# Two-layer AdaLN block on one core: the routing of the first expert stage in smaller pieces, and another order at the first expert tile

## What is computed

```
h = layernorm(x) * (1 + cb) + sb
logits = h @ w_router.T                    # 8 experts
probs = softmax(logits); vals, idx = top_k(probs, 2)
gates = sum(one_hot(idx) * vals)
acc = gelu(h @ Ws1.T + bs1) @ Ws2.T + bs2  # shared expert
acc = acc + sum_e gates[e] * (gelu(h @ W1[e].T + b1[e]) @ W2[e].T + b2[e])
x = x + gb * acc / sqrt(1.25)
```

## Time and profile before

| | |
|---|---|
| runs, us | 971.08, 972.5, 970.03 |
| profiled execution, us | 971.25, its span 969.4, granted clock 0.915 |
| busy in the span | PE 85%, DVE 77%, ACT 63%, POOL 49% |
| attention / first feed-forward / rest | to 480 / 480 to 720 / from 720 |
| chain that ended last | PE 44%, DVE 21%, POOL 13%, issue 11%, ACT 6% |
| mean of one: activation L1307, rounding L1313, subtraction L1442 | 689, 632, 739 ns |
| rank matmuls L459, 16 in all | 386 ns median |
| pieces of the chain: L1028 x2, L1033 x8, L1017 x4 | 1.05, 1.09, about 0.6 us |

### The profile page before, as it was taken

How to read it: one execution, slowest core, us unless ns; L and a number is a source line. 1 busy time by engine, 2 the same in 40 slices (tenths; PEclk the granted TensorE clock), 3 DMA queues, 4 the chain that set the end, 5 groups by cost and what they waited for, 6 DMA issues and landing times.

```text
span 969.4 us, 14044 instructions
## 1 busy us (share of the span) xinstructions
PE 825.5 (85%) x4566; PEld 438.3 (45%) x4566; DVE 746.9 (77%) x1560; ACT 614.3 (63%) x1097; POOL 477.8 (49%) x783
## 2 busy tenths in 40 slices
PE   5499999999988988797896999899962937899996
PEld 4232223323312222222374777787751525676664
DVE  6598888888899878882277688878839776999971
ACT  1128888888867867576385677667733754576541
POOL 4702564737366666346364067775658308314221
PEclk9659999999999999899599899999987957899998
DMA  6834736475647374202104166666533100000001
GB/s 200 189 85 154 177 122 167 131 157 146 142 124 166 112 179 112 86 24 106 62 29 170 35 242 213 232 220 205 189 120 145 26 8 1 0 1 1 1 34 54
DMA packets 45076, 110.77 MB, mean 114 GB/s; under 512 B 7806, under 2 KB 20606, under 8 KB 39494
## 3 DMA queue, kind: packets, MB, share of 16 engines
q1 hardware_dynamic: 39436, 98.33, 34.6%
q0 software_dynamic: 4992, 10.36, 3.1%
q10 hardware_dynamic: 576, 1.19, 0.4%
HBM read 57.65 MB, written 51.03 MB: 112 GB/s over the span
## 4 chain that ended last, share of the span: by engine, by line
PE 44%; DVE 21%; POOL 13%; issue 11%; ACT 6%; DMA 3%; SPq 1%; POOLq 0%; ACTq 0%; DVEq 0%
PE PS L1073 11%; POOL yd L1278 9%; PE PS L1062 8%; PE PS L1046 6%; DVE mx L896 5%; DVE cb L2334 3%; PE PS L1028 1%; PE PS L319 1%; PE PS L1083 1%; PE PS L320 1%; PE PS L321 1%; PE PS L2429 1%; PE PS L1017 1%; POOL Gl L1270 1%; ACT E L808 1%
## 5 line engine op out<-in xcount | busy, mean ns | idle before, releaser
L896 DVE TENSOR_REDUCE mx<-PS 128x2 f32<-128x1024 f32 x256 | 305.5, 1220 | 60.4 <-PE PS L1046 58.5
L808 ACT ACTIVATE E<-PS 128x512 f32<-128x512 f32 x512 | 272.4, 597 | 70.7 <-PE PS L1062 66.5
L1062 PE MATMUL PS<-Q,K 51*128 51x512 bf16 x512 | 167.6, 399 | 15.4 <-ACT E L808 7.3
L1046 PE MATMUL PS<-K,Q 48*128 48x512 bf16 x512 | 144.2, 413 | 27.2 <-DVE mx L896 15.7
L1073 PE MATMUL PS<-E,V 128*18 128x512 f32 x1024 | 142.1, 629 | 0.0
L1062 PEld LDWEIGHTS PS<-Q,K 51*128 51x128 bf16 x512 | 37.5, 95 | 175.9 <-ACT E L808 98.8
L1278 POOL DMA_INDIRECT yd<-yt,goes x92 | 96.1, 1045 | 42.3 <-issue 23.7
L1442 DVE TENSOR_TENSOR Gl<-Gf,Gh 128x512 fp32r<-128x512 f32 x117 | 84.7, 739 | 25.7 <-ACT Gh L1313 21.4
L510 POOL DMA_INDIRECT xs<-HT,pos x64 | 64.0, 1001 | 72.6 <-ACT E L808 41.3
L1307 ACT ACTIVATE Gf<-PS,WR 128x512 f32<-128x512 f32 x92 | 63.3, 689 | 42.1 <-PE PS L321 30.4
L2334 DVE SCALAR_TENSOR_TENSOR cb<-ye,gt,cb 128x128 f32<-128x128 f32 x224 | 62.4, 356 | 0.0
(11 more groups left out here) (421 smaller groups left out, 1830.6 us busy)
## 6 DMA issues: line engine op xcount, KB each, us to landing
WR<-wsd SPq DMA_DIRECT2D x23, 1028.0 KB
xs<-zero SPq DMA_DIRECT2D x8, 2112.0 KB, 7.2
wsd<-wsp SPq DMA_DIRECT2D x8, 1024.0 KB, 4.1
Q<-dqk SPq DMA_DIRECT2D x16, 384.0 KB
K<-dqk SPq DMA_DIRECT2D x16, 384.0 KB
HT<-xs SPq DMA_DIRECT2D x23, 264.0 KB
dqk<-SPL SPq DMA_DIRECT2D x31, 192.0 KB, 2.8
stage<-in_w SPq DMA_DIRECT2D x9, 516.0 KB
```

The lines of the kernel that those rows point to most:

```text
L808: e.activation(E[:, m % 4, n % 4], PS[:, bank["exp", n], :], ACT.Exp).then_inc(*k.inc("exp", n))
L896: e.tensor_reduce(mx[:, 2 * s % 96:2 * s % 96 + 2], PS[:, o:o + 2, :], AX.X, ALU.max, negate=True).then_inc(*k.inc("max", s))
L1046: return e.matmul(PS[:, o + n % 2, :], Q[r, b % 3, h // 2, qt * P:(qt + 1) * P], K[r, b % 3, h // 2, :], start=True, stop=True)
L1062: e.matmul(PS[:, o, :], K[r, b % 3, h // 2, kt * P:(kt + 1) * P], Q[r, b % 3, h // 2, :], start=True, stop=True).then_inc(*k.inc("exp_mm", n))
```

## The change

Routing functions are cut into pieces of one to three operations, and the pieces get steps of their own. The operations are fewer: subtracting the best logit comes first, so that "is the best" is a comparison with zero joined to the weighting; the second mask is added to the first by TensorE's accumulation; running totals carry over from group to group inside the scan, by one more element per expert that is zero in the mask `one`. The groups become 16, 8, 4 and 4 tiles (before: 12, 8, 8, 4). Group 0 is routed in batch 5 (before: 4), group 1 in batch 7, steps 14 to 26 (before: 6), group 2 in batch 7 from step 42. Scatters: tiles 0 to 7 in batch 6 and 8 to 21 in batch 7 (before: six in 5, six in 6, eight in 7, two at its end). At the first expert tile SyncE loads one weight set, waits for the scatters, loads the tokens, then the other two weight and token sets; its transposes move from step (5, 3) to (6, 1), and both roundings two steps later.

```diff
-GROUP0 = {0: (0, 12), 1: (12, 20), 2: (20, 28), 3: (28, 32)}
+GROUP0 = {0: (0, 16), 1: (16, 24), 2: (24, 28), 3: (28, 32)}
+        def dve_best_a(e, k, g):
+            L, w, a, c = group(g)
+            k.wait_ge("lgt", c // 4 - 1)
+            chain(k, e.tensor_reduce(w[:, 4, :, 0], L, AX.X, ALU.max))
+            e.tensor_tensor(L, L, over8(w[:, 4, :, 0]), ALU.subtract).then_inc(*k.inc("v"))
+        def dve_best_b(e, k, g):
+            chain(k, e.scalar_tensor_tensor(w[:, 2], L, 0.0, desc(w), ALU.is_ge, ALU.mult))
+            chain(k, e.tensor_reduce(HT[:, a:c, 129], w[:, 2], AX.X, ALU.max))
+            e.tensor_tensor(w[:, 0], w[:, 2], over8(HT[:, a:c, 129]), ALU.is_equal).then_inc(*k.inc("v"))
+        def dve_second_a(e, k, g):
+            chain(k, e.scalar_tensor_tensor(w[:, 3], w[:, 0], -3.0e38, L, ALU.mult, ALU.add))
+            e.tensor_reduce(w[:, 4, :, 3], w[:, 3], AX.X, ALU.max).then_inc(*k.inc("lgx", g))
...
             for i, m in enumerate(("before", "ones")):
-                r = e.matmul(PS[:, o, 256 * i:256 * i + 8 * (c - a)], W[m], w[:, 2].rearrange("p t e -> p (t e)"),
-                             start=True, stop=True)
+                for x in range(2):
+                    r = e.matmul(PS[:, o, 256 * i:256 * i + 8 * (c - a)], W[m], w[:, x].rearrange("p t e -> p (t e)"),
+                                 start=x == 0, stop=x == 1)
...
-                    if b >= 5:
-                        paced(b, 0, SENT[b], SENT[b] + 2)
-                        paced(b, 9, SENT[b] + 2, SENT[b] + 4)
+                    if b == 6:
+                        paced(b, 0, 0, 2)
+                        paced(b, 9, 2, 4)
+                    if b == 7:
+                        paced(b, 0, 8, 12)
+                        paced(b, 9, 12, 14)
...
-                    if b >= 5:
-                        paced(b, 36, SENT[b] + 4, SENT[b] + 6)
+                    if b == 6:
+                        paced(b, 36, 4, 8)
+                    if b == 7:
+                        paced(b, 30, 14, 18)
                     wsplit(b + 1)
                     if b == 7:
-                        paced(b, 48, SENT[b] + 6, SENT[b] + 8)
+                        paced(b, 44, 18, 20)
+                        paced(b, 50, 20, 22)
...
-                scatter(e, k, 20, 22)
...
+                        if (b, i) == (5, 24):
+                            act_exp(e, k, 0)
+                        if (b, i) == (7, 18):
+                            act_exp(e, k, 1)
+                        if (b, i) == (7, 46):
                             act_exp(e, k, 2)
...
-                for n in range(NS, NS + 3):
-                    load_w(n)
+                load_w(NS)
                 k.wait_ge("scatter", NT - 1)
                 k.wait_ge("xt_mm", 2)
-                for n in range(NS, NS + 3):
+                load_x(NS)
+                for n in range(NS + 1, NS + 3):
+                    load_w(n)
                     load_x(n)
...
-                for u, first in ((0, 22), (7, 24), (11, 26), (15, 28), (18, 30)):
-                    k.wait_ge("gelu", u)
-                    scatter(e, k, first, first + 2)
+                k.wait_ge("gelu", 0)
+                scatter(e, k, 22, 24)
+                k.wait_ge("gelu", 1)
+                scatter(e, k, 24, 28)
+                k.wait_ge("gelu", 13)
+                scatter(e, k, 28, 32)
...
-                        if fc == 0 and n + 1 < NTILE:
+                        if fc == (2 if n + 1 == NS else 0) and n + 1 < NTILE:
                             xh(n + 1)
...
-                        if fc == 1 and n + 1 < NTILE:
+                        if fc == (3 if n + 1 == NS else 1) and n + 1 < NTILE:
                             xl(n + 1)
...
-                        if fc == 3 and n + 2 < NTILE:
+                        if (n, fc) == (NS - 1, 1):
+                            xtr(NS)
+                        if fc == 3 and n + 2 < NTILE and n + 2 != NS:
                             xtr(n + 2)
```

More of the change, by code:

```diff
@@ L34 @@
 ROW = 132
-GROUP0 = {0: (0, 12), 1: (12, 20), 2: (20, 28), 3: (28, 32)}
+GROUP0 = {0: (0, 16), 1: (16, 24), 2: (24, 28), 3: (28, 32)}
+WIDE = max(c - a for a, c in GROUP0.values())
 def width(pack):
@@ new lines, in dve_second_b, with dve_second_c @@
+        def dve_second_b(e, k, g):
+            L, w, a, c = group(g)
+            k.wait_own("lgx")
+            chain(k, e.tensor_tensor(w[:, 2], w[:, 3], over8(w[:, 4, :, 3]), ALU.is_equal))
+            e.tensor_tensor(w[:, 2], w[:, 2], desc(w), ALU.mult).then_inc(*k.inc("picked", g))
+        def dve_second_c(e, k, g):
+            L, w, a, c = group(g)
+            k.wait_own("picked")
+            chain(k, e.tensor_reduce(w[:, 4, :, 2], w[:, 2], AX.X, ALU.max))
+            e.tensor_tensor(w[:, 1], w[:, 2], over8(w[:, 4, :, 2]), ALU.is_equal).then_inc(*k.inc("chosen", g))
@@ L449, in dve_gates, with dve_gates_b @@
             chain(k, e.tensor_reduce(w[:, 4, :, 5], L, AX.X, ALU.add))
[L450 to L453, removed]
+            e.reciprocal(w[:, 4, :, 4], w[:, 4, :, 5]).then_inc(*k.inc("share", g))
+        def dve_gates_b(e, k, g):
+            L, w, a, c = group(g)
+            k.wait_own("share")
+            chain(k, e.tensor_tensor(HT[:, a:c, 130], w[:, 4, :, 6], w[:, 4, :, 4], ALU.mult))
+            e.tensor_tensor(HT[:, a:c, 131], w[:, 4, :, 4], HT[:, a:c, 130], ALU.subtract).then_inc(*k.inc("gates", g))
         def pe_ranks(e, k, g, o):
@@ L475, in dve_starts @@
+            e.tensor_copy(w[:, 3], PS[:, o, 0:8 * n].rearrange("p (i e) -> p i e", e=8))
+            e.tensor_copy(tot[:, :, 1:n + 1], PS[:, o, 256:256 + 8 * n].rearrange("p (i e) -> p e i", e=8)).then_inc(*k.inc("rk", g))
         def dve_starts(e, k, g):
[L477 to L481, removed]
@@ L482, in dve_starts @@
-            k.wait_own("rk")
[L483 to L487, removed]
-            chain(k, e.tensor_tensor(inc, inc, tot, ALU.subtract))
-            e.tensor_tensor(over, over, bs.unsqueeze(2).to_broadcast([P, 8, n]), ALU.add).then_inc(*k.inc("v"))
@@ L491, in dve_places @@
-        def dve_places(e, k, g):
-            L, w, a, c = group(g)
-            tot, inc, r = counted(g)
-            k.wait_own("v")
-            chain(k, e.tensor_tensor(w[:, 3], r.rearrange("p (i e) -> p i e", e=8), inc.rearrange("p (e i) -> p i e", e=8), ALU.add))
-            for x in range(2):
-                chain(k, e.tensor_tensor(w[:, x], w[:, x], w[:, 3], ALU.mult))
-                chain(k, e.tensor_reduce(posf[:, x, a:c], w[:, x], AX.X, ALU.add))
+            L, w, a, c = group(g)
@@ new lines, in dve_starts @@
+            n = c - a
+            inc = by_expert(rk, g)
+            k.wait_own("rk")
+            chain(k, e.tensor_tensor_scan(rk[:, 0:8 * n + 8], one[:, g, 0:8 * n + 8], tt[:, g % 2, 0:8 * n + 8], 0.0, ALU.mult, ALU.add))
+            e.tensor_tensor(w[:, 3], w[:, 3], inc[:, :, 0:n].rearrange("p e i -> p i e"), ALU.add).then_inc(*k.inc("base", g, 0))
+            if g + 1 < len(GROUP0):
+                e.tensor_copy(by_expert(tt[:, (g + 1) % 2], g + 1)[:, :, 0], inc[:, :, n]).then_inc(*k.inc("base", g, 1))
@@ L499, in dve_places, with dve_places_a, dve_places_b @@
+        def dve_places_a(e, k, g):
+            L, w, a, c = group(g)
+            k.wait_own("base")
+            e.tensor_tensor(w[:, 0:2], w[:, 0:2], w[:, 3].unsqueeze(1).to_broadcast([P, 2, c - a, 8]), ALU.mult).then_inc(
+                *k.inc("placed", g))
+        def dve_places_b(e, k, g):
+            L, w, a, c = group(g)
+            k.wait_own("placed")
+            chain(k, e.tensor_reduce(posf[:, :, a:c], w[:, 0:2], AX.X, ALU.add))
             e.tensor_copy(pos[:, :, a:c], posf[:, :, a:c]).then_inc(*k.inc("pos", g))
```

166 lines of the change are left out of this document (96 added, 70 removed).

## The result

| | before | after |
|---|---|---|
| median, us (range, runs) | 970.56 (968.88 to 972.5, 4) | 958.87 (956.77 to 960.56, 4) |
| ratio, 95% interval | | 0.9866 (0.9838 to 0.9895) |
| profiled execution / span, us | 971.25 / 969.4 | 958.48 / 956.6 |
| stage start of the feed-forward part (its first transposes), us | 480.43 | 471.52 |

Faster by 11.7 us, where 38 were forecast; 958.9 lies above the range. The windows of the changed kernel, cut at the same exponentials as the earlier trace rows, say where: batch 4, 5, 6, then batch 7 to the last product with the normaliser, and its last 24 us. The numbers are those of the earlier trace rows: stretch, length, busy PE, PEld, DVE, ACT and POOL, granted clock, DMA.

The account below looks back on a forecast made before the run. TensorE sets the pace in batches without routing; bursts of VectorE routing, a ScalarE wait in batch 7 and the first expert tile's load cost time. From 971.25 us, -10.3 -0.5 -9.7 +1.0 -10.7 -8.1 = -38.3 gives 933.0; range 924 to 951.

Parts of the forecast that it names:

- batch 4: Attention batch 4 loses all its routing and falls from 57.1 to 46.8 us: -10.3.
- batch 5: Attention batch 5 gets routing group 0 in short places, its scatters leave: 50.5 us, -0.5 (ends -4.2 and +3.2).
- batch 6: Attention batch 6 loses routing, gets eight scatters, a Pool wait and half clock: 48.6 us, -9.7 (ends -15 and -4).
- first expert tile: Feed-forward start: 6.6 us idle and 2.3 of half clock go, new 1.8 wait for Hl: -8.1 (ends -10 and 0).
- everything after: Everything after the first expert tiles is untouched and counted at nothing.
- rival (a): Routing bursts cost the same anywhere: batch 5 takes 54.2, ScalarE still waits in batch 7 with half clock: 947 us; chance 0.12.
- forecast wait of TensorE for Pool in step 54: In batch 6, eight scatters delay Pool's preparation of batch 7's maxima; TensorE waits 3.3 us, with half clock after.
- Batch 7 up to group 2: Twelve scatters take 15.2 us of Pool, about in time for TensorE; hidden states 1 late: +1.0 (ends 0 and +4).
- The rest of batch 7: From group 2's exponentials on, ScalarE's 3.8 us wait goes and full clock stays: -10.7 (ends -3.8 and -12).
- (b): Pool's late preparation stops TensorE in step 22 of batch 7; half clock from there: 949 us; chance 0.10.
- (c): The new order starves the first expert tile (Hl and the next tile's load late), so it gives nothing: 941 us; chance 0.09.
- (d): Slower: batch 5's many short waits drop the clock, which does not return before the attention ends: 990 us; chance 0.04.

Follow-up runs that it names:

- first ladder: Changed kernel plus four, eight and twelve extra scatters of zeros at the start of batches 2, 3 and 4: 936.74 us, on another chip 972.48.
- third version in fours: Changed kernel, scatters in fours; late in batch 7 tiles 16, 17 after exponential 42, then weight split, 18, 19 after 50, 20, 21 after 62: 937.95 us, ratio 0.9667.
- chip B: One of five chips used for follow-ups; kernel before 965.21 us beside three kernels with extra Pool work (936.74, 953.45, 938.05); scatters in fours throughout took 928.60.
- three ladders: Changed kernel with extra scatters or other Pool work at the start of batches 2, 3 and 4, in three forms: 936.74, 953.45 and 938.05 us.
- A, C and D: Three of five follow-up chips; the kernel before ran beside the others on each; the unchanged changed kernel took 958.21 us on C.
- chip E: One of five follow-up chips; ran two versions of the changed kernel with scatters in fours: 937.57 us (ratio 0.9645) and 937.95 (0.9667).
- second ladder: Changed kernel plus twelve scatters with landing waits after each four (batch 2), twelve in fours (batch 3), twenty Pool copies (batch 4): 953.45 us, on another chip 972.31.

## Why the prediction was wrong

The sum by its terms, span against span, 38.3 forecast and 12.8 had:

| step | forecast | measured |
|---|---|---|
| batch 4 | -10.3 | -10.3 |
| batch 5 | -0.5 | -1.8 |
| batch 6 | -9.7 | -7.8 |
| batch 7 | +1.0 and -10.7 | +11.0 |
| first expert tile | -8.1 | -4.3 |
| everything after | 0 | +0.4 |

**Batch 4**, right. **Batch 5**: the short places were hidden better than put, with clock 1.00; inside the ends, and rival (a) is refuted. The floor of 48.3 for VectorE was too high: it was busy 45.76.

**Batch 6**: near, for another reason in this execution. The forecast wait of TensorE for Pool in step 54 did not come; the stops behind the run of eight came in its place (VectorE 3.11 us idle before 388.06, "remote"). In the first ladder, where nothing was held up, the transpose waited 2.63 us for Pool (forecast 3.3) and the batch took 48.0 (forecast 48.6).

**Batch 7 up to group 2** is the step that failed. The prediction wrote "Pool issues twelve scatters in a row", counted them as 15.2 us of Pool's time, and asked only who waits for Pool; +1.0, at most +4. It left out what a run of scatters does to engines that do not wait for Pool. The trace of before had a hint: in its own run of eight (362 to 373) ScalarE idled 1.57 us before 371.04, VectorE 2.34 before 372.42, and once more together at 373.9, "remote". I had read that stretch only for who waits for Pool. The runs put the price at 5.2 for eight and 9.3 for twelve in a batch of its own, and at 9.8 for twelve in batch 7 of the kernel before. The changed kernel has twelve and then eight and eight more in batch 7: from step 8 to the last exponential it took 57.5 us, against 40.4 in the first ladder, where nothing was held up. How much of these 17.1 the second and third run cost, and how much half clock that came for another reason, is not taken apart.

**The rest of batch 7**: VectorE's seven operations before the release took 3.8 us instead of 1.9, since one stood beside Pool's subtraction. The Trainium skill (GPSIMD Engine Reference, section Key points) says that GpSimd shares its SBUF interfaces with VectorE and contends with VectorE instructions that have two SBUF inputs. The trace agrees: this operation, of two SBUF inputs, took 2.39 us, and those after it 0.19. The prediction had priced one such hit at about 1 us of ScalarE's wait; the wait was 0.99. That is not what cost the 10.7. The clock fell at 444.3, before that wait began at 445.8, behind the run of scatters of tiles 14 to 17 (432 to 442), and stayed down for 20 us; that is the lower end of this term, "if the clock falls all the same". The first ladder and the third version in fours show four exponentials at 2.38 us up to the last, as forecast. From step 8 of batch 7 to the next stage the first ladder took 50.64 us against 60.00 before: -9.4, with -9.7 forecast. So the working of batch 7 stood, but only for an execution without the hold-up. That its 936.7 is close to 933 is partly luck: beside the kernel before on its own chip it is 28.5 us faster, not 38.

**First expert tile**: the idle time of 6.6 and the half clock went, and the new wait for Hl is 1.76 (forecast 1.8). The term missed 2.9 us to a joint stop at the end of twelve scatters (the transposes of tile 4 came 9.16 us earlier than before, at 495.21 against 504.37, those of tile 5 only 6.30), and 0.9 of small things.

**The rivals**: (a) falls with batch 5. (b), half clock from the middle of batch 7, named 949 and is nearest, but in the changed kernel by another cause: its transpose of step 22 (426.03) did not wait for Pool. On chip B, without the hold-up, (b) did come, in one of three executions: Pool was 1.1 us late in all three ladders, where the prediction had it within 0.2, and in the second half clock followed and cost 9.0 us (49.4 against 40.4). (c) and (d) did not come. Of the signs that were named, those of batch 4, the length of batch 5 and those of tile 7 came as put; the wait for Pool in step 54 and the full clock to the last exponentials did not.

**What stays open**: by which path scatters hold up the signals of other engines, and why none of the four profiles from chip B shows it, when all thirteen from the chip of the result and from A, C and D do (that of the kernel before has only a short wait of the kind, 0.81 us). The changed kernel itself was not run on chip B, so chip and chance are not told apart. On chip E only fours were run, and their two profiles show no hold-up. Every time on record has a granted clock beside it, so every execution was being recorded; whether the recording has a part in the hold-up was not tried. How far apart fours must be was not settled either.

## What to carry to other kernels

Price a Pool scatter by what it does to the others, not only by Pool's time: look in the trace for places where two or three engines stop and resume together with no releaser that was busy, and see what Pool issues there. Keep such instructions in fours, with other work of Pool between, and check in the trace that they really left in fours: an engine that is late runs through its pauses. A wait for the landing also keeps the hold-up away, but the wait itself made Pool late and cost 7.1 us. As the rows in one scatter don't count, fewer and larger ones may help; no run tried it. Before naming a cause for lost time, look what the stopped engine waited for: in the second ladder 7 us that looked like the hold-up were a wait for Pool. When a group of work is moved later, its transfers are packed tighter into what is left of the stage, and that belongs in the sum.

## What the runs showed of the hardware

Runs of scatters on Pool delay the other engines: 0, 5.2 and 9.3 us for four, eight and twelve at 1.27 us apart (the half clock after a stop included), and for twelve about the same whether each has 32, 64 or 128 rows, or 4 bytes per row (11.0, 11.1 and 9.5). Copies that keep Pool busy for 13.5 us cost nothing, and twelve with a wait for the landing after each four made no hold-up. The hold-up showed in all thirteen profiles from the chip of the result and from A, C and D, apart from the kernel before's own (0.81 us), and in none of four from chip B; one program took 936.7 us there and 972.5 on chip C.

In batch 7, where maxima have ended, a wait of TensorE of 1.1 us for Pool was followed by 24 us of half clock in one execution and by none in two. The same stretch of work took 49.4 us in the first case and 40.4 in the others.
